# Lead expert from half the tokens, eight buffers for x, short empty rows and a new hand-over in a convolution with routed experts

## The reference

```python
def _L0_cond_ref(x, w, b):          # depthwise causal convolution, 8 taps
    K = w.shape[0]
    D = x.shape[-1]
    y = jax.lax.conv_general_dilated(x, w, window_strides=(1,), padding=[(K - 1, 0)], feature_group_count=D, dimension_numbers=('NWC', 'WIO', 'NWC'))
    return y + b

def _L0_ffn_ref(x, w_router, w_experts):
    logits = jnp.einsum('bsh,eh->bse', x, w_router)
    idx = jnp.argmax(logits, axis=-1)
    all_out = jnp.einsum('bsh,efh->bsef', x, w_experts)
    out = jnp.take_along_axis(all_out, idx[:, :, None, None], axis=2)[:, :, 0, :]
    return out
x = x + _L0_ffn_ref(_L0_cond_ref(x, cond_2048[:, None, :], L0_cond_b), L0_ffn_w_router, L0_ffn_w_experts)
```

## Time and profile before

| | |
|---|---|
| median of three runs | 563.32 us (561.74 to 563.69) |
| the profiled execution: time, span, mean granted clock | 566.44 us, 564.3 us, 0.973 |
| PE busy, PEld busy | 510.3 us (90%), 439.8 us (78%) |
| DVE, ACT, POOL busy | 284.0 us, 148.0 us, 141.1 us |
| L703, 1680 matmuls | 387.5 us busy, 19.6 us idle before them |
| L661, 1024 matmuls | 122.3 us busy, 27.7 us idle before them |
| chain that ended last | PE 77%, DMA 10%, DVE 5%; L703 62%, L661 15%, loads of x_t 5% |
| transfers | 134.52 MB, 238 GB/s over the span; q10: 26208 packets, 14.0% |

### The profile page before, as it was taken

How to read it: one execution, slowest core, us unless ns; L and a number is a source line. 1 busy time by engine, 2 the same in 40 slices (tenths; PEclk the granted TensorE clock), 3 DMA queues, 4 the chain that set the end, 5 groups by cost and what they waited for, 6 DMA issues and landing times.

```text
span 564.3 us, 8973 instructions
## 1 busy us (share of the span) xinstructions
PE 510.3 (90%) x2740; PEld 439.8 (78%) x2741; DVE 284.0 (50%) x351; ACT 148.0 (26%) x255; POOL 141.1 (25%) x150
## 2 busy tenths in 40 slices
PE   5967999797459979999789999999999999999995
PEld 5967889796348768888678888888888888888884
DVE  4907255381699043424787623428424832376581
ACT  2432332433610010103456100115103400061430
POOL 1700605032035122222021242211222123211313
PEclk9997999999969979999989999999999999999998
DMA  8896987969947985554998964558664976469535
GB/s 335 308 364 157 333 228 254 294 202 399 285 121 303 338 228 180 164 171 116 365 339 257 385 196 133 168 160 327 196 192 141 340 215 187 117 237 316 186 112 185
DMA packets 59473, 134.52 MB, mean 238 GB/s; under 512 B 11712, under 2 KB 31680, under 8 KB 59456
## 3 DMA queue, kind: packets, MB, share of 16 engines
q1 hardware_dynamic: 18416, 60.96, 32.5%
q0 software_dynamic: 14832, 54.27, 27.1%
q10 hardware_dynamic: 26208, 19.07, 14.0%
HBM read 94.62 MB, written 39.65 MB: 238 GB/s over the span
## 4 chain that ended last, share of the span: by engine, by line
PE 77%; DMA 10%; DVE 5%; issue 3%; ACTq 1%; another core or an unknown queue 1%; SPq 1%; ACT 1%; POOL 0%; DVEq 0%; POOLq 0%
PE ps L703 62%; PE ps L661 15%; DMA xs<-x_t 5%; DMA w_raw<-experts 2%; DMA ids_all<-y_sorted 2%; DMA router<-router_t 1%; ACTq L264 1%; SPq L290 1%; DVE w_sb L560 0%; DVE y_cols L569 0%; DVE x_row L582 0%; DVE logits L460 0%; ACT w_sb L362 0%; DVE xs L439 0%
## 5 line engine op out<-in xcount | busy, mean ns | idle before, releaser
L703 PE MATMUL ps<-w_sb,ys 128*128 128x512 f32 x1680 | 387.5, 393 | 19.6 <-issue 10.7
L703 PEld LDWEIGHTS ps<-w_sb,ys 128*128 128x128 f32 x1680 | 319.2, 190 | 87.3 <-issue 15.4
L661 PE MATMUL ps<-mats,xs 128*128 128x128 f32 x1024 | 122.3, 281 | 27.7 <-DVE xs L439 15.9
L661 PEld LDWEIGHTS ps<-mats,xs 128*128 128x128 f32 x1024 | 119.7, 197 | 29.3 <-DVE xs L439 17.0
L569 DVE STREAM_TRANSPOSE y_cols<-y_blk 128x1024 f32<-128x1024 f32 x36 | 44.7, 1243 | 154.9 <-PE ps L703 138.1
L374 ACT CAST ys<-y_cols 128x1024 fp32r<-128x1024 f32 x36 | 37.9, 1052 | 274.2 <-DVE y_cols L569 271.6
L560 DVE TENSOR_TENSOR w_sb<-w_raw,w_sb 128x1024 fp32r<-128x1024 f32 x64 | 73.4, 1220 | 26.5 <-ACT w_sb L362 22.9
L362 ACT CAST w_sb<-w_raw 128x1024 fp32r<-128x1024 f32 x64 | 62.3, 1048 | 36.6 <-issue 16.5
L439 DVE COPY xs<-xs 56x1008 f32<-56x1008 f32 x48 | 33.0, 688 | 71.8 <-DMA xs<-x_t 71.1
L771 POOL DMA_INDIRECT out<-x_row,idx x35 | 41.9, 1197 | 107.0 <-DVE x_row L582 103.4
L356 ACT COPY rows<-ps 128x448 f32<-128x448 f32 (+1 forms) x76 | 39.6, 521 | 89.1 <-PE ps L661 80.4
(11 more groups left out here) (78 smaller groups left out, 29.2 us busy)
## 6 DMA issues: line engine op xcount, KB each, us to landing
w_raw<-experts SPq DMA_DIRECT2D x64, 512.0 KB, 6.6
y_blk<-y_sorted ACTq DMA_DIRECT2D x144, 128.0 KB
xs<-x_t SPq DMA_DIRECT2D x48, 256.0 KB
xs<-x_both SPq DMA_DIRECT2D x16, 512.0 KB
y_sorted<-empty SPq DMA_DIRECT2D x1, 4160.0 KB, 16.0
y_blk<-y_sorted SPq DMA_DIRECT2D x8, 128.0 KB
x_row<-x_rows,idx POOLq DMA_INDIRECT x36
ids_all<-y_sorted ACTq DMA_DIRECT2D x36, 1.0 KB
```

What stands on the lines that cost most here:

```text
L661: mm = nc.tensor.matmul(to, xs[:, n % X_RING, s % PACK, :], mats[:, s, :].rearrange("p (u n) -> p u n", n=SIDE), start=(s == sets[0]), sto ...
L703: mm = nc.tensor.matmul(out_ps[k][:, f * HALF:(f + 1) * HALF], ys[k][:, a, c, :], w_sb[:, c, b, f * HALF:(f + 1) * HALF], start=(c == 0 an ...
```

## The change

The parts, in the order of the program:
- Taps, router and the unit matrix come as one tensor `factors`, in three loads (2, 6 and 8 packs) on SP's queue. The ranking matrix comes as bf16 bits within `cst`; POOL's conversion of it goes.
- x has eight buffers. `load_x` is shared code, called by SP alone. `ys1` now lies over two of the buffers.
- Of the empty rows only the 16 words that hold the token number are written, 64 bytes for each of 1024 rows, by ACT's queue at the start.
- `find_lead` is run after two quarters instead of three. The lead expert's first two slots are rows 0 to 255 of it; the third starts 128 rows before the smaller of 384 and its count after three quarters (`third_slot`), and the table takes its rest from there.
- The weight chunks follow x packs 50 to 55, 56 and 58, not 60 and on.
- Each of the eight scatters of the first two quarters waits for one more pack of the next quarter's conv.
- ACT evicts the logits' part first; DVE sums 15 of 19 banks of a quarter before its end (`sum_most`) and four at the end.
- The order of the hand-over is new on DVE, ACT and SP. SP loads the rows of slots 0 to 4.

Numbers, the third slot and POOL's scatters:

```diff
+X_RING = 8
+DOUBLED = PACKS
...
 LAST = GROUPS - 1
-FIRST = LAST * GT // EXPERTS // P
+FIRST = (LAST - 1) * GT // EXPERTS // P + 1
 MOST_SLOTS = (TOKENS + EXPERTS * (P - 1)) // P
 RING = 2
...
-                V.tensor_scalar(lead_i[:, :], const(C_SPLIT, FIRST), full_row, None, ALU.add).then_inc(first_known, 1)
+                V.tensor_scalar(lead_i[:, 0:2], const(C_SPLIT, 2), full_row, None, ALU.add).then_inc(first_known, 1)
+
+            def third_slot():
+
+                step(V.tensor_tensor(count, base, const(C_BASE), ALU.subtract))
+                step(V.scalar_tensor_tensor(out=done, in0=count, scalar=float(FIRST * P), in1=lead, op0=ALU.min, op1=ALU.mult))
+                step(V.tensor_reduce(one[:, 6:7], done, AX.X, ALU.add))
+                step(V.tensor_scalar(one[:, 6:7], one[:, 6:7], full_row, -float(P), ALU.add, ALU.add))
+                V.tensor_copy(lead_i[:, 2:3], one[:, 6:7]).then_inc(third_known, 1)
```

SP's program:

```diff
+                return sp.value_load(lead_i[0:1, n:n + 1], min_val=0, max_val=EXPERTS * TOKENS - P)
 
             def load_raw(e, c):
                 src = experts[bass.ds(e, 1), :, c, :].rearrange("e p f -> (e p) f")
                 sp.dma_start(w_raw[:, c, :], src).then_inc(raw_in[c], 16)
 
-            sp.dma_start(taps[:, 0:2 * PACK, :], taps_t[:, 0:2 * PACK, :]).then_inc(taps_in[0], 16)
-            load_x(0)
-            load_x(1)
-            load_x(2)
-            sp.dma_start(taps[:, 2 * PACK:, :], taps_t[:, 2 * PACK:, :]).then_inc(taps_in[1], 16)
-            sp.dma_start(router[:, 2 * PACK:, :], router_t[:, 2 * PACK:, :]).then_inc(router_part_in[1], 16)
-            for n in range(3, X_RING + 2):
-                load_x(n)
-            sp.dma_start(count_f[:, :], consts[:, N_CONST:]).then_inc(count_in, 16)
-            for n in range(X_RING + 2, PACKS):
-                load_x(n)
-
-            sp.wait_ge(empty_ready, 2)
-            sp.dma_start(y_sorted.rearrange("(e r) n -> r e n", e=EXPERTS)[0:P, :, :],
-                         empty[:, :].unsqueeze(1).to_broadcast([P, EXPERTS, ROW])).then_inc(empty_out, 16)
-            early = GROUPS * PACKS - 4
-            for n in range(PACKS, early):
-                load_x(n)
+            load_factors(0)
+            load_x(sp, 0)
+            load_x(sp, 1)
+            load_factors(1)
+            load_x(sp, 2)
+            load_x(sp, 3)
+            load_factors(2)
+            early = (LAST - 1) * PACKS + X_RING + 10
+            for n in range(4, early):
+                load_x(sp, n)
 
...
             sp.wait_ge(mats_ready, PACKS)
-            sp.wait_ge(empty_out, 16)
-            sp.wait_ge(before_ready, 1)
-            for k in range(4):
-                load_raw(e, k)
-                load_x(early + k)
-            for c in range(4, HC):
-                load_raw(e, c)
+            chunks = iter(range(HC))
+            for k, n in enumerate(range(early, GROUPS * PACKS)):
+                load_x(sp, n)
+                if k < 6 or k % 2 == 0:
+                    c = next(chunks, None)
+                    if c is not None:
+                        load_raw(e, c)
 
             sp.wait_ge(y_out[0], 2 * TPG * 16)
             sp.wait_ge(y_out[1], TPG * 16)
-            load_first(0)
-            load_first(1)
+            for t in range(RING):
+                load_y(sp, lead_row(t), t, ids_all[:, t:t + 1, :])
+
+            sp.wait_ge(third_known, 1)
+            row = lead_row(2)
+            sp.wait_ge(y_blocks, 1)
+            load_y(sp, row, 0, ids_all[:, 2:3, :])
 
             sp.wait_ge(table_ready, 1)
+            sp.wait_ge(y_out[1], 2 * TPG * 16)
+            for t in range(FIRST, FIRST + RING):
+                row = sp.value_load(tab_i[0:1, 0, t:t + 1], min_val=0, max_val=EXPERTS * TOKENS - P)
+                sp.wait_ge(y_blocks, t - 1)
+                load_y(sp, row, t % RING, ids_all[:, t:t + 1, :])
             loads = sp.value_load(one_i[0:1, 1:2], min_val=0, max_val=EXPERTS - 1)
```

ACT's:

```diff
+            act.dma_start(cst[:, :], consts).then_inc(const_in, 16)
             act.wait_ge(warm_zero, 1)
             nc.scalar.activation(warm[:, 1:2], warm[:, 0:1], ACT.Identity)
+            act.wait_ge(empty_ready, 1)
+            act.dma_start(y_sorted.rearrange("(e r) n -> r e n", e=EXPERTS)[0:P, :, H:],
+                          empty[:, :].bitcast(F32).unsqueeze(1).to_broadcast([P, EXPERTS, ROW - H])).then_inc(empty_out, 16)
...
                 if b == 0 and g >= 2:
 
                     act.wait_ge(y_out[g % 2], TPG * 16)
+                    act.wait_ge(most_sum, g - 1)
...
-                nc.scalar.copy(to, conv_bank(n)[:, 0:m * SIDE].rearrange("p (c j i) -> p j c i", j=PHASES, i=CH))
-                nc.scalar.copy(part[:, g % 2, b, :], conv_bank(n)[:, PER_BANK * SIDE:]).then_inc(conv_out, 1)
+                nc.scalar.copy(part[:, g % 2, :, b], conv_bank(n)[:, PER_BANK * SIDE:]).then_inc(part_out, 1)
...
+                if b == BANKS - 1:
+                    high_y(0, 0)
                 evict(LAST, b)
-                if spare <= b < spare + HC:
-
-                    act.wait_ge(conv_mm, sets_done(LAST, 2 * PACK * (b - spare + 1)))
-                    high(0, b - spare)
-            high_y(0, 0)
-            act.wait_ge(y_blocks, 1)
-            load_y(act, lead_row(2), 0, ids_all[:, 2:3, :])
+                while ready and 2 * PACK * (ready[0] + 1) <= bank_sets(b)[-1] + 1:
+
+                    act.wait_ge(conv_mm, sets_done(LAST, 2 * PACK * (ready[0] + 1)))
+                    high(0, ready.pop(0))
             high_y(1, 1)
+
+            act.wait_ge(gemm_chunk, HC)
             high_y(2, 0)
-
+            high_y(FIRST, FIRST % RING)
             act.wait_ge(table_ready, 1)
-            act.wait_ge(y_out[1], 2 * TPG * 16)
-            load_slot(FIRST, FIRST % RING)
-            load_slot(FIRST + 1, (FIRST + 1) % RING)
-            high_y(FIRST, FIRST % RING)
             load_slot(FIRST + 2, (FIRST + 2) % RING)
```

DVE's, PE's rank of the last quarter and POOL's scatter:

```diff
+
+                dve.wait_ge(part_out, g * BANKS + MOST_BANKS)
+                V.tensor_reduce(most[:, :], part[:, g % 2, :, 0:MOST_BANKS], AX.X, ALU.add).then_inc(most_sum, 1)
...
+                dve.wait_ge(part_out, (g + 1) * BANKS)
+                flat = logits[:, :, :].rearrange("p t e -> p (t e)")
+                V.tensor_reduce(flat, part[:, g % 2, :, MOST_BANKS:], AX.X, ALU.add).then_inc(logit_sum, 1)
                 dve.wait_ge(logit_sum, g + 1)
+                dve.wait_ge(most_sum, g + 1)
+                step(V.tensor_tensor(flat, flat, most[:, :], ALU.add))
...
             dve.wait_ge(const_in, 16)
-            dve.wait_ge(taps_in[0], 16)
-            dve.wait_ge(router_part_in[0], 16)
-            for n in range(PACKS):
-                if n == 2:
-                    dve.wait_ge(taps_in[1], 16)
-                    dve.wait_ge(router_part_in[1], 16)
-                build_mats(n)
+            sum_most(0)
             for g in range(1, GROUPS):
                 n = g * PACKS
-                for k in range(4):
+                for k in range(5):
                     double(n + k)
                 choose(g - 1)
-                for k in range(4, 7):
-                    double(n + k)
+                double(n + 5)
+                double(n + 6)
                 place_rows(g - 1)
-                if g == LAST:
-                    find_lead()
-                for k in range(7, PACKS):
-                    double(n + k)
-
-            for c in range(HC):
-                low(0, c)
+                double(n + 7)
+                if g < LAST:
+                    if g == LAST - 1:
+                        find_lead()
+                    for k in range(8, PACKS):
+                        double(n + k)
+                else:
+                    third_slot()
+                    for c in range(4):
+                        low(0, c)
+                        double(n + 8 + 2 * c)
+                        double(n + 9 + 2 * c)
+                if g < LAST:
+                    sum_most(g)
+
+            low(0, 4)
             turn_blocks(0, 0, 1)
+            low(0, 5)
             turn_blocks(1, 1, 1)
+            sum_most(LAST)
+            low(0, 6)
             low_y(0, 0)
             choose(LAST)
+            low(0, 7)
             low_y(1, 1)
             place_rows(LAST)
+            turn_blocks(2, 0, 2)
             count_slots()
+            slot_starts()
+            low_y(2, 0)
+            residual(0, 0, 1)
             slot_table()
-            turn_blocks(2, 0, 2)
-            residual(0, 0, 1)
-            low_y(2, 0)
             turn_blocks(FIRST, FIRST % RING, FIRST // RING + 1)
             residual(1, 1, 1)
...
                     mm.then_inc(gemm_chunk, 1)
-                    if nth is None and c == 1:
+                    if nth is None and c == 2:
                         rank(LAST)
...
+                    if g < LAST - 1:
+
+                        pool.wait_ge(conv_mm, pack_done((g + 1) * PACKS + 3 + j))
```

161 lines of the change are left out of this document (85 added, 76 removed).

## The result

Measured beside the kernel before on one chip, the changed kernel takes 547.95 us (median of 4 runs, 545.76 to 548.92), the one before 563.51: ratio 0.9724, interval 0.9688 to 0.976. It is faster by some 15.6 us, half of the 31.9 forecast. The profiled execution took 548.22, its span is 546.3.

The account below looks back on a forecast made before the run. PE was taken as busy 90%, with 35 expert products the floor and only its waits to save. First product 136.0 + 34.8 to slot 3 + 0.5 wait + 361.1 behind = 532.4 us, against 564.3; range 522 to 546.

Parts of the forecast that it names:

- Start and second quarter: First quarter ends at 36.8 us, start 0.8 us earlier; without 10.4 us of empty-row transfers the 7.7 us wait goes.
- From pack 42 to 47 each pack has 1.1 + 1.3 = 2.4 us of transfers: Before the last quarter, x pack plus weight chunk take 2.4 us, putting x 3.6 us more behind, 8.5 in all.
- 2.5 + 2.0: Waits in conv: 2.5 us for late x (0 to 15.5) and 2.0 without a cause; conv ends at 128.3.
- The rival of five packs at 4.9 us: Transfers bound the last quarter: five x packs at 4.9 us against 1.8 add 15.5; total 544, chance 0.12.
- About at conv's end: Hand-over: slot 0's rows come right behind the last x, 2.2 us of transfer, landing about when conv ends.
- the work behind them: Hand-over: transposes, subtractions, long sum and y's low part take 7.7 us (4 to 12); first product at 136.0.
- Slot 3: Table at +25.6 us after the first product, rows at +31; slot 3 waits at most 0.5 us, against 4.2.
- The rival in which its rows land late: Slot 3's rows land 11.8 us after the last issue: 9 us of wait plus half clock, total 543, chance 0.18.
- Tail: Behind slot 3: 363.9 us becomes 361.1, as 2.8 us of half-clock loss goes; the 4.8 us weight wait stays.
- Slower: ACT stands before all eight late weight chunks, 4.9 us each, PE stops: 39 us more, total 568, chance 0.03.
- conv to 143 and hand-over to 12: Upper bounds in the working: conv ends between 123.8 and 143 us; the hand-over takes 4 to 12 us.

Follow-up runs that it names:

- late chunks: Changed kernel with the lead expert's weight chunks issued from pack 60 of x on and behind all of x, as before the change: 541.89 us, ratio 0.9626.
- the hand-over run: Changed kernel with hand-over work that needs no rows put ahead of slot 0's rows on DVE and ACT: 542.15 us, ratio 0.9586.

## Why the prediction was off

- **Start and second quarter: right.** The first matmul is at 5.77 (5 to 6 forecast), nothing waits near 37, and from the start to the last quarter nothing holds PE for copies of x. The 64 B pieces had no visible price.
- **Last quarter: the failed term.** "From pack 42 to 47 each pack has 1.1 + 1.3 = 2.4 us of transfers" took the pace of each kind of load by itself and added them. In one queue they took 3.3. That made x late and the ranking wait. The waits it had as 2.5 + 2.0 were 4.3 + 1.8, and 3.2 for the lower clock, which it had at nothing: 9.3, 4.8 of the 5.3 by which conv was late. Shown by: the rate returns with loads into 128 partitions; the ranking's wait goes when the chunks are moved out of the stretch, and is 1.07 us with them in another queue. The rival of five packs at 4.9 us has the right place and resource, but needs 15.5 us; what came was a third.
- **"About at conv's end": the second failed term.** The forecast's rows of slot 0 were bound to the last x, not to the scatter. The scatter waits for the row numbers, which DVE makes behind the quarter's seventh copy of x, late too; it was issued at 110.61, had its first packet 6.2 us later and ended past 132. The rows were turned at 138.81, 5.2 us after conv. That they don't follow x shows best with the chunks on ACT's queue: conv ended at 124.9 and they were turned at 135.59. The size of the work behind them was right (7.85 for 7.7), though the long sum took 1.1 for 1.8. What was missed is that this work stood behind the rows by DVE's order; moved ahead, 4 us go where the rows are the later ones.
- **Slot 3: right.** Its table is ready (line 586) at 172.59, 25.9 us behind the first product (25.6 forecast), and its wait is 0.96 us, with the clock at 1.00 there. The rival in which its rows land late fell.
- **Tail: 2.2 us too short.** From slot 3 to the end of the wait for weights it is 82.35 us for 83.69 before, 1.3 less, where 2.8 were taken for the half clock; and what stands behind that wait is 0.8 longer than before (280.96 for 280.17).
- **Slower: no.** ACT's stand before a chunk did not come where the chunks were early, and came with 3.4 to 4.9 us where they were late: it is real, but one chunk long, since ACT's waits for the later ones (1.2 to 1.8 us with late chunks) did not hold PE.
- **The range** (522 to 546) missed for want of a case with both failed terms at once. Each has its own bounds in the working, conv to 143 and hand-over to 12, but the range ended where one of them alone would. From conv's end to the first product it was 13.1 us, outside even its own bound.

Open: why the chunks are slowed along with x (apart in two queues both still moved only 292 GB/s), by which rule a backlog in one queue delays a scatter in another, and what moved conv's end by 3 us in the hand-over run.

## What to carry to other kernels

Price two kinds of loads in one queue by their rate together, not by the sum of each alone: the slower kind can set the pace of both. Look also at what stands ahead of the load that is wanted first; a second queue gave x its part back though the rate hardly rose. A load moved earlier is paid where it now stands, and again by whatever waits in another queue behind it, here the scatter on which the next stage rests. At a hand-over, see which input comes last and put the work that doesn't need it first: that took 4 us off where the rows were last, and nothing where the weights were.

## What the hardware showed

- A scatter's first packet came 1.6 us after its instruction with the other queues empty, 2.2 with SyncE's queue at 56%, and 6.2 with it at 102.6% and 236 GB/s; from 117 to 130 us, with both served, it was 405 GB/s.
- The 1024 pieces of 64 B for the empty rows landed 8.7 us after their issue, in a stretch (0 to 10 us) that moved 2.7 MB in all. The first matmul stands at 5.77, and at 6.00 in the run with whole empty rows, which has no such pieces at the start: writes under 512 B, which by the Trainium skill (DMA: Bandwidth & Descriptors, Specifications) are a read, a change and a write, had no price that this trace shows.
- The clock was at 1.00 before PE's wait of 4.3 us and at its lower level (0.50) from 104 to 110 behind it. The wait of 0.96 us before slot 3 left it at 1.00, and so did six waits of up to 1.96 us, 9.8 in all, in the run that chooses after three copies.
